# Feed-forward weights loaded in one transfer each, the down weight in pieces during attention, and two convolution groups one step earlier

## The reference

```python
y  = cond_mix(x, cond)                      # per batch entry a 32x32 channel mix, from an MLP on cond
x  = x + attention(y; Wq, Wkv, Wo, bo)      # causal, 32 positions, 32 heads of 16, 8 key/value groups
c  = conv1d(x, weight, groups=4, taps=9)    # along the 512 features, plus a shift from cond
h1 = c @ (w1 + 2*B1@A1).T;  h3 = c @ (w3 + 2*B3@A3).T        # 512 -> 1376, LoRA of rank 16
x  = x + (silu(h1) * h3) @ (w2 + 2*B2@A2).T                  # 1376 -> 512
```

## Time and profile before

| | us |
|---|---|
| median of 3 runs | 604.81 (600.99 to 606.08) |
| the profiled execution, its time | 603.86 |
| its span, first to last instruction | 602.1 |
| PE busy | 579.9 (96%) |
| DVE, ACT, POOL busy | 240.8, 172.7, 182.0 |
| mean granted PE clock | 0.987 |
| moved by DMA | 59.22 MB |

### The profile page before, as it was taken

How to read it: one execution, slowest core, us unless ns; L and a number is a source line. 1 busy time by engine, 2 the same in 40 slices (tenths; PEclk the granted TensorE clock), 3 DMA queues, 4 the chain that set the end, 5 groups by cost and what they waited for, 6 DMA issues and landing times.

```text
span 602.1 us, 7725 instructions
## 1 busy us (share of the span) xinstructions
PE 579.9 (96%) x3035; PEld 463.6 (77%) x3035; DVE 240.8 (40%) x340; ACT 172.7 (29%) x296; POOL 182.0 (30%) x131
## 2 busy tenths in 40 slices
PE   9996999979998979999999999999999999999997
PEld 6994888757776658888778888768888767888885
DVE  1431544589999853111453111325111144111112
ACT  3561212556654343333221111113111112111110
POOL 3445491778999865544400000000000000000000
PEclk9997999989999989999999999999999999999999
DMA  6997747645467677000008300004600001200001
GB/s 239 276 208 219 241 149 262 174 134 137 122 178 176 190 253 165 0 1 0 1 0 224 73 0 1 1 1 140 155 0 0 0 0 70 70 1 0 1 1 70
DMA packets 70798, 59.22 MB, mean 98 GB/s; under 512 B 45136, under 2 KB 61904, under 8 KB 69648
## 3 DMA queue, kind: packets, MB, share of 16 engines
q1 hardware_dynamic: 69904, 57.43, 34.2%
q10 hardware_dynamic: 864, 1.38, 0.6%
HBM read 40.94 MB, written 16.79 MB: 96 GB/s over the span
## 4 chain that ended last, share of the span: by engine, by line
PE 75%; DMA 13%; SPq 6%; POOL 2%; DVE 2%; issue 1%; ACT 1%; ACTq 0%; DVEq 0%; POOLq 0%
PE twin L1317 41%; PE twin L1338 20%; DMA f_sb<-in_f 6%; PE twin L1143 5%; DMA x_dram<-rows 4%; SPq L467 2%; DMA rows<-x_dram 2%; PE twin L1215 2%; PE twin L1283 2%; SPq L497 2%; PE twin L1163 1%; PE twin L1176 1%; PE twin L1132 1%; POOL wo_lo L626 1%; SPq L446 1%
## 5 line engine op out<-in xcount | busy, mean ns | idle before, releaser
L1034 DVE TENSOR_TENSOR gate<-twin,gate 128x512 f32<-128x512 f32 (+1 forms) x44 | 30.4, 691 | 246.2 <-PE twin L1317 246.2
L1317 PE MATMUL twin<-c_hi,f_lo 128*128 128x512 f32 (+1 forms) x352 | 96.7, 397 | 4.2 <-POOL f_lo L671 4.2
L1317 PE MATMUL twin<-c_hi,f_hi 128*128 128x512 f32 (+1 forms) x352 | 96.3, 396 | 0.0
L1317 PE MATMUL twin<-c_lo,f_hi 128*128 128x512 f32 (+1 forms) x352 | 95.6, 394 | 0.0
L1317 PEld LDWEIGHTS twin<-c_hi,f_lo 128*128 128x128 f32 (+1 forms) x352 | 65.6, 187 | 20.4 <-POOL f_lo L671 4.6
L1317 PEld LDWEIGHTS twin<-c_hi,f_hi 128*128 128x128 f32 (+1 forms) x352 | 66.0, 188 | 15.9 <-issue 0.3
L1317 PEld LDWEIGHTS twin<-c_lo,f_hi 128*128 128x128 f32 (+1 forms) x352 | 65.9, 187 | 15.7
L857 ACT ACTIVATE gate<-twin 128x512 f32<-128x512 f32 (+1 forms) x44 | 26.3, 598 | 171.5 <-PE twin L1317 171.5
L1338 PE MATMUL twin<-f_lo,gate_hi 128*128 128x512 f32 (+1 forms) x176 | 68.5, 389 | 0.0
L860 ACT CAST gate_hi<-gate 128x512 fp32r<-128x512 f32 (+1 forms) x44 | 27.3, 620 | 128.7 <-DVE gate L1034 128.7
L1338 PE MATMUL twin<-f_hi_head,gate_hi 128*128 128x512 f32 x128 | 50.2, 392 | 0.0
(11 more groups left out here) (150 smaller groups left out, 818.1 us busy)
## 6 DMA issues: line engine op xcount, KB each, us to landing
f_sb<-in_f SPq DMA_DIRECT2D x8, 688.0 KB, 24.5
x_dram<-resid_stage SPq DMA_DIRECT2D x16, 256.0 KB, 2.2
rows<-x_dram SPq DMA_DIRECT2D x16, 256.0 KB, 3.4
q_t<-q_dram SPq DMA_DIRECT2D x8, 512.0 KB, 4.2
x_dram<-rows SPq DMA_DIRECT2D x16, 256.0 KB, 3.4
rows<-x_dram SPq DMA_DIRECT2D x8, 512.0 KB, 4.4
out<-rows SPq DMA_DIRECT2D x12, 256.0 KB, 2.0
f_sb<-in_f SPq DMA_DIRECT2D x1, 2560.0 KB, 11.5
```

Of the source, the lines that this page charges most:

```text
L1034: dve.tensor_tensor(gate[0:w, h % 2, :], up_bank[2 * (h % 2) + 1][0:w, :], gate[0:w, h % 2, :], ALU.mult).then_inc(gate_ready, 1)
L1317: mm = pe.matmul(bank[0:w, :], f[:, c, :], c_part[:, c, :], start=(n == 0 and c == 0), stop=(n == 2 and c == DC - 1))
```

## The change

Three things are changed.

1. Each up weight (`f3`, `f1`; 128 rows of 22,016 bytes) is loaded by one transfer over all 128 partitions, where four transfers of 32 partitions each were issued. So that one transfer can do it, the order of rows is another: partition x\*32+l holds row 4l+x of the source. The factor copies and the convolution's reading of the windows follow that order (a step of two elements where 32 neighbours were read).
2. The down weight is loaded in four transfers (chunks 0 to 3, 4 to 7, 8 and 9, and the last of 96 rows) at steps 7, 15 and 18 of the attention loop, where two transfers were issued at step 17.
3. Groups 0 and 1 of the first convolution are computed at step 15 and turned at step 16; groups 2 and 3 stay.

```diff
-        a_part = up_part[2 * S:3 * S, 0:2 * D].rearrange("k (x r l) -> k x r l", r=2, l=S)
-        a_up = up_sb[:, 0:2 * D].rearrange("k (x l r) -> k x r l", r=2, l=S)
+        a_part = up_part[2 * S:3 * S, 0:2 * D].rearrange("k (y x l) -> k y x l", x=BT, l=S)
+        a_up = up_sb[:, 0:2 * D].rearrange("k (y l x) -> k y x l", x=BT, l=S)
...
-        f2_loads = [(f2_sb[:, 0:HC - 1, :], f2[0:(HC - 1) * P, :].rearrange("(c p) d -> p c d", p=P)),
-                    (f2_sb[0:HW[-1], HC - 1, :], f2[(HC - 1) * P:HID, :])]
+        f2_loads = [(f2_sb[:, a:b, :], f2[a * P:b * P, :].rearrange("(c p) d -> p c d", p=P))
+                    for a, b in ((0, 4), (4, 8), (8, HC - 1))]
+        f2_loads += [(f2_sb[0:HW[-1], HC - 1, :], f2[(HC - 1) * P:HID, :])]
...
             for f_sb, f in ((f3_sb, f3), (f1_sb, f1)):
-                for part in range(4):
-
-                    sp.dma_start(f_sb[part * S:(part + 1) * S, :, :],
-                                 f.rearrange("(h l r) c j -> h r l c j", h=2, r=2)[part // 2, part % 2])\
-                        .then_inc(ffn_loaded, 16)
+                sp.dma_start(f_sb[:, :, :].rearrange("p c j -> p (c j)"),
+                             f.rearrange("(l x) c j -> x l (c j)", x=BT)).then_inc(ffn_loaded, 16)
...
-                if n == QUADS + 1:
+                if n == 7:
+                    load_f2(0)
+                if n == QUADS - 1:
 
                     for half in range(2):
                         sp.wait_ge(k_loaded[half], 16 * G * BLOCKS)
+                    load_f2(1)
+                if n == QUADS + 2:
+
                     sp.wait_ge(v_spread, 2 * BT * BLOCKS)
-                    for dst, src in f2_loads:
-                        sp.dma_start(dst, src).then_inc(f2_loaded, 16)
+                    load_f2(2)
+                    load_f2(3)
...
-                if n == QUADS + 1:
-                    for g in range(GROUPS):
+                if n in (QUADS, QUADS + 1):
+                    for g in range(2):
+                        g += 2 * (n - QUADS)
                         turn_conv(0, g, first_conv_bank[g])
...
-                    pe.wait_ge(ffn_loaded, 16 * 8)
+                    pe.wait_ge(ffn_loaded, 16 * 2)
...
                     mm = pe.matmul(bank[part, :], conv_sb[:, g, :, :, :].rearrange("k h r o -> k (h r o)"),
-                                   near[g][:, :, half * S:(half + 1) * S], start=True, stop=True)
+                                   near[g].rearrange("k b (l h) -> k h b l", h=2)[:, half], start=True, stop=True)
...
-                if n == QUADS:
-
-                    pe.wait_ge(conv_packed, 1)
-                    pe.wait_ge(scores_turned, QUADS)
-                    for g in range(GROUPS):
+                if n in (QUADS - 1, QUADS):
+
+                    pe.wait_ge(scores_turned, n)
+                    for g in range(2):
+                        g += 2 * (n - QUADS + 1)
                         convolve(0, g, first_conv_bank[g])
```

More of the change, by code:

```diff
@@ L315, in adaln_attention_ffn @@
         out_slot = [out_spare[:, :]] + [rows[:, t, :] for t in range(TILES - 1)]
-        a_part = up_part[2 * S:3 * S, 0:2 * D].rearrange("k (x r l) -> k x r l", r=2, l=S)
-        a_up = up_sb[:, 0:2 * D].rearrange("k (x l r) -> k x r l", r=2, l=S)
+        a_part = up_part[2 * S:3 * S, 0:2 * D].rearrange("k (y x l) -> k y x l", x=BT, l=S)
+        a_up = up_sb[:, 0:2 * D].rearrange("k (y l x) -> k y x l", x=BT, l=S)
         b_part, b_up = up_part[S:2 * S, :], up_sb[:, 2 * D:2 * D + HID]
         a_down, b_down = down_sb[:, 0:HID], down_sb[:, HID:HID + D]
-        a_up_s_rows = a_up_s[:, :, :].rearrange("k f (x r l) -> k (f x) r l", r=2, l=S)
+        a_up_s_rows = a_up_s[:, :, :].rearrange("k f (y x l) -> k (f y) x l", x=BT, l=S)
         q_stage = (q_t, q_odd)
@@ L499, in load_near, with load_f2 @@
                         .then_inc(near_loaded[g // 2], 16)
+            def load_f2(part):
+                dst, src = f2_loads[part]
+                sp.dma_start(dst, src).then_inc(f2_loaded, 16)
             def load_conv_shift(i):
```

## The result

The changed kernel takes 657.08 us (median of 4 runs, 654.06 to 663.82); the kernel before, timed on the same chip, 604.99 (600.99 to 606.08). The ratio is 1.089, with a 95% interval of 1.078 to 1.100: 52 us slower. The profiled execution is the longest of the four, 663.82 us (span 662.0); that is 60.0 above the profiled execution of before (603.86).

The account below looks back on a forecast made before the run. PE was taken as 75% of the path, DMA 13%, with PE waits for the up weights and POOL's low part. 603.86 + 78.7 - 5.6 - 0.9 = 676.1 us; own range 660 to 686, stated range 618 to 686.

Parts of the forecast that it names:

- Four engines: Up weights' load: four outer source steps put only four engines to work; 105.3 us load, 78.7 more; chance 0.43.
- The rivals with sixteen engines: Up weights' load on sixteen engines: faster, 589.4 us, chance 0.19; or half rate, load time unchanged, 597.4, chance 0.05.
- time to landing: Sign at the second up-weight transfer: 100 us or more for the forecast, about 60 first rival, under 30 second.
- the first rival: Up weights' load: four engines apart from each other, 25.4 GB/s each, 28.9 us added, 626.3 in all; chance 0.33.
- At half rate because they meet: Up weights' load: engines on partitions 32 apart share ports in step, so each keeps 13.4 GB/s.
- The clock: First fold and twelve products after the up-weight wait: lower clock costs 2.1 us, paid as before, nothing added.
- The end of attention: Start of feed-forward: down-weight pieces let the last residual load land earlier, ending PE's 4.2 us wait; gain 5.6 us.
- can delay the last residual tiles by 2 us: Down-weight piece at step 15: uses 2 us of the 3.7 between 210 and POOL's 213.7, so costs nothing.
- The piece of step 7: Early down-weight piece in attention: holds queries and keys by up to 3 us, first read two steps later; costs nothing.
- The convolution a step earlier: End of attention: groups 0 and 1 fill PE's 1.36 us wait for DVE; gain 0.9 us, bounds 0 and 1.4.
- Reading every second element: Convolution windows, 64 instructions of 0.22 us: taken as 0; 14 us added if the reading halved the speed.
- the second rival: Up weights' load: sixteen engines, over before 47.8 us, whole 8.0 us wait gone, 589.4 in all; chance 0.19.

Follow-up runs that it names:

- eight engines for eight outer steps: Sorted-rows kernel with up-weight rows stored so one transfer reads 8 outer steps of 16 rows: 621.55 us, 1.031 of the kernel before.
- the plain copy: Changed kernel with up-weight rows already sorted in memory, so each load is one transfer of 128 plain rows: 591.28 us, 0.978 of the kernel before.
- the second profile: Changed kernel timed once more with nothing altered: 658.01 us, 1.091 of the kernel before; its profiled execution took 655.88 us.
- The two-engine kernels: Changed kernel, two 32-partition blocks of each up weight in one transfer, the others singly: pair on partitions 0 to 63 671.28 us, on 32 to 95 641.38.
- 591.28 with SP's queue: Changed kernel with up-weight rows sorted in memory, SP still issuing all down-weight pieces: 591.28 us, 0.978 of the kernel before.
- 589.61 with ACT's: Sorted-rows kernel with all but the first down-weight piece issued by ACT at step 15: 589.61 us, 0.979 of the kernel before.

## Why the prediction was right, point by point

**Four engines: right.** The weights' packets keep 4.0 engines busy, eight engines for eight outer steps and nearly all for the plain copy settle it. The rivals with sixteen engines fall with it. The page lists no time to landing for the new transfers, which the prediction had named as a sign; by the packets both together took 89.2 us, between the forecast's 100 and the first rival's 60.

**At half rate because they meet: right in kind, the term too large.** The prediction priced the load at 105.3 us and the added wait at 78.7. Measured: 89.2 us and 60.3 (85.4 and 57.4 in the second profile). The mis-sized term is the rate that was held constant, "13.4 GB/s that they have now". It begins near it (15.0) but climbs to 20.1. The two-engine kernels show that the two halves of one 64 slow each other and partitions across its edge don't. They also show why the rate climbs: a row takes 818 ns when its engine meets no other and about twice that when it does, and the mixture changes. In the changed kernel's load no row between 28 and 38 us takes under 830 ns and 16 of 28 take 1,500 or more; between 74 and 84 us it is 10 and 10 of 33. So the engines meet less as they go on. That they do because they get out of step with time is my reading; the trace does not say which partition a packet goes to. The sixteen engines of the earlier trace rows had 13.4 over the whole 27 us (236 of the 238 rows that start then take 1,500 ns or more); they all write the same 32 partitions, so getting out of step would not help them, which I had not thought through. For the same reason the nearest row for the rate was not near enough.

So the truth lay between the forecast and the rival of four engines apart (626.3). The median of 657.1 lies under the forecast's own range of 660 to 686; it is inside the stated one because that was drawn to hold both cases of four engines. Against the profiled execution (663.8) the forecast of 676.1 is 12.3 too high, and two misses partly cancel in that: the wait was put 18.4 too high, while the clock took 1.0 more and the other parts gave 5.2 less than forecast.

**The clock: 1.0 us more than counted.** I took the cost of the lower clock as paid already. It is 1.48 + 4.91 against 0.62 + 2.75, 3.0 us instead of 2.1; in the second profile it is 2.4. PE worked 6.0 us at 0.50 before the clock rose, 4.6 in the second profile and 3.9 before the change; why it differs is open. The waiting and the clock give 61.3; what is left of 60.0 is the other parts' -1.3.

**The end of attention: right as a mean, wrong in the profiled execution.** The forecast was 5.6 us. The down-weight parts are worth 4.5 us, by the run without them, and the changed kernel's second profile has gained 5.7 together with the convolution (57.4 of waiting and 0.3 of clock, less 52.0), where the forecast for both was 6.5. In the first profile the step that failed is "can delay the last residual tiles by 2 us": it delayed them by 6.97 - 3.22 = 3.7, and the last two pieces, issued behind them, came later by as much. Then the low part and the folds are both late. In the second profile the load behind the same store follows it 6.2 us after the store's issue and not 7.0, and nothing waits. That it can fall either way with one and the same code shows how thin the slack of 3.7 us is. The piece of step 7 cost nothing, as forecast: PE's wait for the spread keys is 0.7 us where it was 0.4.

**The convolution a step earlier: right.** 0.9 forecast, 0.9 between two medians, but inside their spread; the profile's wait (5.8 against 4.7) is the better witness, from one execution each.

**Reading every second element: near nothing, not nothing.** 0.02 us for an instruction; a feed-forward block of the middle took 95.39 us against 95.24, which makes 0.6 us in all. The step that the prediction quoted as free costs 3% of the matmul here (612 ns for 592), and the measurement decides. The bound of 14 us was far off.

**Sorting the rows** was not in the change, but the second rival's number, 589.4, is about what one gets when the load really runs on sixteen engines: 591.28 with SP's queue, 589.61 with ACT's.

## What to carry to other kernels

Before merging several transfers into one, write down the outermost count of source and destination: with 4 and 128 there are four engines at work, whatever the bytes, and rows sorted in memory give one load all sixteen (389 GB/s here against 62 to 96). Don't let engines that run side by side write partitions 32 apart inside one 64: a row took some 1,650 ns while they met and 818 when they did not. A large load issued ahead of a chain of small stores and loads that wait for each other delays the chain: here 1 MB made one store land 3.7 us later, and all that stood behind it on the queue with it. Count the chain's slack first, or issue the piece earlier, from a queue that has nothing of the chain behind it; that version had the lowest median here, but within the spread.

## What the runs showed that I had not expected

- An engine takes 818 ns for a row of 22,016 bytes into one partition when no other writes the other half of the same 64, and about twice that when one does. Two engines on partitions 0 to 31 and 32 to 63 had rows of 1,313 to 1,665 ns between 44 and 51 us; two on 32 to 63 and 64 to 95 had 818 in row after row. Four engines in one transfer: from 15.0 to 20.1 GB/s each within 70 us.
- A transfer on four engines ends with the slowest of them: one was through at 97 us, the last at 113.8.
- The same kernel loads the same weights in times that differ by 3.7 us between two executions (89.2 and 85.4; waits of 66.2 and 63.3). The kernel with the sorted load spreads less as a whole (590.2 to 592.5).
- A moving operand that is read with a step of two float32 elements: 612 ns for a matmul of 128 x 512 that took 592.
